# A gated delta-rule decoder layer on one core: the first normalisation pipelined over batches, head 0's key projections begun per batch

## The reference

```
xn = layernorm(x)
q, k, v = silu(causal_conv4(xn @ Wqkv))         # 16 heads of 128, 4 taps per channel
z    = xn @ Wz
beta = sigmoid(xn @ Wb);  g = softplus(xn @ Wa + dt_bias) * -exp(A_log)
per head and token:  M = exp(g) M;  M += k (v - kM) beta;  o = q M
x = x + (rmsnorm(o) * norm_w * silu(z)) @ Wout
x = x + cross attention(layernorm(x), ctx)
x = x + one of 8 experts of rank 64(layernorm(x))
```

## Time and profile before

| | |
|---|---|
| runs | 2026.42, 2033.64, 2031.08 us, median 2031.08 |
| profiled execution | span 2031.7 us from the first to the last instruction; no other time of that execution is given |
| TensorE | busy 1915.2 us, 94% of the span; mean granted clock 0.958 |
| VectorE | busy 1128.8 us, 56% |
| ScalarE | busy 934.1 us, 46% |
| GpSimd | busy 743.1 us, 37% |
| before head 0's L606 | 90.13 us, 4.4% of the span |

### The profile page before, as it was taken

One profiled execution on the slowest core, in us unless ns is written; L12 is line 12 of the kernel. 1 busy time (PEld: TensorE's weight loads), 2 busy tenths in 40 slices (PEclk: granted clock), 3 DMA queues, 4 the chain that ended last, 5 costly groups with the idle time before them and its releaser, 6 DMA issues.

```text
span 2031.7 us, 45678 instructions
## 1 busy us (share of the span) xinstructions
PE 1915.2 (94%) x16962; PEld 1561.4 (77%) x16962; DVE 1128.8 (56%) x2048; ACT 934.1 (46%) x2987; POOL 743.1 (37%) x1143
## 2 busy tenths in 40 slices
PE   5899999999999999999999998999997799999999
PEld 3688888888888888888888887888886565656574
DVE  5656565665656575656656665657563442534433
ACT  2455554646464555646464645555563321213121
POOL 1255453636363554536363535445452000000000
PEclk9899998999998999989999999989997899999999
DMA  3011111112010111111120101021114513121110
GB/s 101 16 33 32 33 40 25 34 30 42 22 38 22 38 32 33 39 25 37 28 43 22 38 22 38 23 41 34 31 24 144 146 36 93 42 83 52 55 27 21
DMA packets 220196, 87.10 MB, mean 43 GB/s; under 512 B 138320, under 2 KB 204240, under 8 KB 219280
## 3 DMA queue, kind: packets, MB, share of 16 engines
q1 hardware_dynamic: 220048, 84.83, 16.4%
HBM read 57.28 MB, written 27.53 MB: 42 GB/s over the span
## 4 chain that ended last, share of the span: by engine, by line
PE 49%; issue 25%; POOL 10%; DVE 7%; ACT 4%; DMA 3%; SPq 1%; POOLq 1%; DVEq 0%; ACTq 0%
PE bank L558 17%; PE bank L858 4%; PE bank L808 3%; DVE vT L1406 2%; POOL blkT L1774 2%; PE bank L817 2%; PE bank L770 2%; POOL prod L1770 2%; PE bank L759 2%; PE bank L678 2%; ACT vv L1074 2%; PE bank L802 2%; POOL k_tok L1740 2%; PE bank L824 1%; DMA blkT_d<-blkT 1%
## 5 line engine op out<-in xcount | busy, mean ns | idle before, releaser
L558 PE MATMUL bank<-x_hi,w_hi 128*128 128x512 f32 x1024 | 433.5, 423 | 13.4 <-DVE vT L1406 7.1
L558 PE MATMUL bank<-x_hi,w_lo 128*128 128x512 f32 x1024 | 410.3, 401 | 0.0
L558 PE MATMUL bank<-x_lo,w_hi 128*128 128x512 f32 x1024 | 408.7, 399 | 1.1 <-issue 1.1
L558 PEld LDWEIGHTS bank<-x_hi,w_hi 128*128 128x128 f32 x1024 | 197.9, 193 | 56.1 <-issue 13.9
L558 PEld LDWEIGHTS bank<-x_hi,w_lo 128*128 128x128 f32 x1024 | 196.7, 192 | 43.8
L558 PEld LDWEIGHTS bank<-x_lo,w_hi 128*128 128x128 f32 x1024 | 197.7, 193 | 33.2 <-issue 1.6
L1406 DVE SCALAR_TENSOR_TENSOR qT<-bank,cw,qT 128x511 f32<-128x511 f32 (+2 forms) x192 | 142.1, 747 | 51.1 <-ACT qT L1041 46.5
L1830 POOL TENSOR_TENSOR rstd<-ve,mhalf 128x1 f32<-128x1 f32 x32 | 17.4, 544 | 386.8 <-DVE ve L1588 386.8
L1406 DVE SCALAR_TENSOR_TENSOR kT<-bank,cw,kT 128x511 f32<-128x511 f32 (+2 forms) x192 | 143.3, 747 | 9.9 <-ACT kT L1041 4.9
L1206 ACT ACTIVATE o_tmp<-bank 128x128 f32<-128x128 f32 x256 | 67.4, 278 | 175.5 <-PE bank L824 175.5
L1406 DVE SCALAR_TENSOR_TENSOR vT<-bank,cw,vT 128x511 f32<-128x511 f32 (+2 forms) x192 | 143.2, 746 | 6.8 <-ACT vT L1041 2.3
(11 more groups left out here) (221 smaller groups left out, 4446.2 us busy)
## 6 DMA issues: line engine op xcount, KB each, us to landing
w_raw<-in_w_heads SPq DMA_DIRECT2D x64, 256.0 KB, 2.8
o_d<-og SPq DMA_DIRECT2D x64, 256.0 KB, 2.6
o_raw<-o_d SPq DMA_DIRECT2D x16, 1024.0 KB, 6.2
x_in<-in_x SPq DMA_DIRECT2D x16, 256.0 KB, 3.3
blkN_d<-nT SPq DMA_DIRECT2D x64, 64.0 KB, 2.1
t<-blkT_d SPq DMA_DIRECT2D x64, 64.0 KB, 2.4
wo_raw<-in_w_out SPq DMA_DIRECT2D x4, 1024.0 KB, 9.1
x_res<-in_x SPq DMA_DIRECT2D x16, 256.0 KB, 2.7
```

The lines of the kernel that those rows point to most:

```text
L558: last = mm(bank[bk][:, :], w[:, kind % 2, d, :], xx[:, d, b * S:(b + 1) * S], start=(n == 0), stop=(n == 3 * ND - 1))
```

## The change

- There are two input buffers: `x_in0`, and `x_in1` on the place of `nT`, which head 0 writes only later. SP loads batch 0 before the small constants, and batches 1 to 3 as the buffers come free, with the weights of K ahead of batch 1 and those of V behind it.
- DVE's `normalise_x` falls into `moments`, `normalise_x` and `low_parts`. The moments of batch b+1 stand between `x_n` and `x_lo` of batch b.
- The transposes go to banks 4 and 5; banks 0 and 1 are the jobs' from the start.
- PE runs per batch: transposes, the token transposes of the batch before, the token products, and the K job of this batch. Its K taps on ACT and K convolutions on DVE stand in the same loop, one batch behind. Weights are split at batches 0 and 1.
- The softplus chain now comes behind the convolutions of K0 to K3 on DVE. On ACT the four `silu` of K follow `tap(0, V_, 0)`.
- All loops of this stage are written out (no `Fori`).

```diff
-    x_in = s0("x_in", [P, NC, D])
+    x_in = [s0("x_in0", [P, NC, D]), at(place["nT"][0], "x_in1", [P, NC, D])]
...
+            for c in range(NC):
+                sp.dma_start(x_in[0][:, c, :], x[0, c]).then_inc(x_loaded[c], 16)
             for dst, src in ((cw_all[:, :, :, :], conv_w), (normw[:, :], norm_w), (wba[:, :, :], w_ba),
                              (alog[:, :], a_log), (dtb[:, :], dt_bias)):
                 sp.dma_start(dst, src).then_inc(small_in, 16)
...
+            def load_batch(b):
+                for c in range(NC):
+                    sp.wait_ge(stat0_step, 2 * NC * (b - 1) + c + 1)
+                    if b >= 2:
+                        sp.wait_ge(xn_done, b * NC - 2 * NC + c + 1)
+                    sp.dma_start(x_in[b % 2][:, c, :], x[b, c]).then_inc(x_loaded[c], 16)
...
             load_weight(0, K_)
+            load_batch(1)
             load_weight(0, V_)
+            load_batch(2)
+            load_batch(3)
...
-            for job in range(AHEAD):
-                if job >= 2:
-                    whole_job(0, job)
+            for b in range(B):
+                transposes(b)
+                if b == 0:
+                    pe.wait_ge(wba_split, 1)
+                else:
+                    token_transposes(b - 1)
+                token_products(b)
+                if b >= 2:
+                    whole_job(0, b)
                 else:
                     pe.wait_ge(wlo_done, 1)
-                    proj(*JOBS[job], JOB_BANK[job])
+                    proj(*JOBS[b], JOB_BANK[b])
+            token_transposes(B - 1)
+            for job in range(B, AHEAD):
+                whole_job(0, job)
...
+            split(0, K_)
+            for kind in (K_, V_, Q_):
+                taps_of(0, kind)
+            for b in range(B):
+                if b + 1 < B:
+                    high_parts(b + 1)
                 tokens(b)
+                if b == 0:
+                    split(0, V_)
+                    act.wait_ge(cw_ready, 3)
+                tap(0, K_, b)
...
+            moments(0)
+            normalise_x(0)
+            moments(1)
+            low_parts(0)
...
+            split(0, K_)
+            for b in range(1, B):
+                normalise_x(b)
+                if b + 1 < B:
+                    moments(b + 1)
+                low_parts(b)
+                if b == 1:
+                    split(0, V_)
+                tokens(b - 1)
+                conv(0, K_, b - 1)
+            tokens(B - 1)
+
+            dve.wait_ge(ba_done, B)
+            dve.wait_ge(small_in, 16 * 5)
+            chain(tt(sp_x[:, :, :], ba[:, :, H:2 * H], by_unit(dtb), ALU.add))
+            conv(0, K_, B - 1)
+            dve.wait_ge(sp_act, 5)
```

More of the change, by code:

```diff
@@ L525, in transposes, with token_products @@
                     for d in range(ND):
-                        last = tr(bank[c % 2][:, d * P:(d + 1) * P], x_n[:, c, d * P:(d + 1) * P], ident[:, :])
+                        last = tr(bank[4 + c % 2][:, d * P:(d + 1) * P], x_n[:, c, d * P:(d + 1) * P], ident[:, :])
                     last.then_inc(xtr_done, 1)
-            def tokens(b):
+            def token_products(b):
                 pe.wait_ge(xlo_done, b * NC + NC)
@@ L543, in tokens @@
                 last.then_inc(batr_done, 1)
[L545 to L550, removed]
             def proj_products(kind, b):
@@ L998, in high_parts @@
                     act.wait_ge(xtr_done, b * NC + c + 1)
-                    fn(x_hi[:, :, bass.ds(b * S + c * P, P)], grid(c % 2), ACT.Copy).then_inc(xhi_done, 1)
+                    fn(x_hi[:, :, b * S + c * P:b * S + c * P + P], grid(4 + c % 2), ACT.Copy).then_inc(xhi_done, 1)
             def tokens(b):
@@ L1365, in by_unit, with dest, conv @@
                 return v[:, :].unsqueeze(1).to_broadcast([P, UNITS, H])
+            def dest(kind, b):
+                return (kT, vT, qT)[kind][:, b, :, :].rearrange("p c t -> p (c t)")
+            def conv(h, kind, b):
+                n = conv_index(kind, b)
+                d = dest(kind, b)
+                for k in range(1, TAPS):
+                    if k == 1:
+                        dve.wait_ge(tap_done, 12 * h + n + 1)
+                    else:
+                        dve.wait_ge(conv_step, 24 * h + 2 * n + k - 1)
+                    stt(d[:, k:S], bank[JOB_BANK[JOBS.index((kind, b))]][:, 0:S - k], cw[:, kind, TAPS - 1 - k:TAPS - k], d[:, k:S],
+                        ALU.mult, ALU.add).then_inc(conv_done if k == TAPS - 1 else conv_step, 1)
+            moments(0)
+            normalise_x(0)
+            moments(1)
+            low_parts(0)
+            dve.wait_ge(wba_hi_done, 1)
+            tt(wba_lo[:, :, :], wba[:, :, :], wba_hi[:, :, :].bitcast(F32), ALU.subtract).then_inc(wba_split, 1)
+            split(0, K_)
[9 more added lines that the diff above has]
+            tokens(B - 1)
             dve.wait_ge(ba_done, B)
@@ L1700, in deviations @@
                 tt(rstd0[:, :], ve0[:, :], minus_half[:, 0:NC], ALU.pow).then_inc(rstd0_done, 1)
-            deviations(0)
-            with pool.Fori(1, B) as b:
+            for b in range(B):
                 deviations(b)
```

80 lines of the change are left out of this document (22 added, 58 removed).

## The result

The changed kernel took 2011.8 us (median of 4 runs, 2008.1 to 2019.3) against 2032.4 us (2026.4 to 2036.7) for the kernel before beside it: ratio 0.9905, 95% interval 0.9876 to 0.9934. The change gains 16 to 19 us. I had forecast 6.8 us and a time of 2024.3 us, so "faster" was right and the time lies outside the range.

What follows compares the result with a forecast made beforehand. TensorE, busy 94% of the span, was taken as the bound, only head 0's start mattering. Terms moved it from 90.13 to 82.95 us; less 0.4 for low clock, gain 6.8: span 2024.9, median 2024.3, range 2017.5 to 2032.0 us.

Steps and rivals of the forecast that it cites:

- The ring of a batch: Batches before head 0: x_n, transposes, x_hi/x_lo, token products, baT, ba in turn; 5.3 us from first transpose to first product.
- the chain from sp_x to the first convolution: Serial softplus steps after the last batch: sp_x to sp_p 3.5 us, then 7.17 to the first convolution, at 75.2 us.
- PE's wait ahead of V2: Before head 0, PE idles over 7 us for V0's convolution; V2 starts cold at 77.65 us and takes 5.3 us.
- Items 1 and 2: Batch 0: early loads bring x_n near 8.4 us; batch 1's moments cancel the 2.3 us gained; first product about 18.2.
- E: Rival: moments ahead of x_lo stall it as much as they save; in all sums for batch 0, no separate chance.
- Item 3: Block 0: 24 products together, 14 at the low clock for 6.1 us, then 10 in 2.4 us; end 26.7 us.
- Items 4 and 5: Batches 1 to 3: 11.15 us each at high clock, plus 1.65 us low-clock cost in two; K3 ends at 63.45.
- rival B: No low stretch in batches 1 to 3: gain 9.8 us, 2021.3, down to 2018 with other blocks partly fast; chance 0.22.
- Sum ahead of head 0: All terms of the prologue together put head 0's start (L606) at 82.95 us instead of 90.13.

Runs made afterwards that it cites:

- The corrected swap: Changed kernel with x_lo, wba_lo and the first weight split of batch 0 ahead of batch 1's moments on DVE, nothing else; ratio 0.9919.
- The second execution: Profiled execution of the changed kernel run again, unchanged, in the second comparison with the kernel before; ratio 0.9922, head 0 starting at 77.18 us.
- the normalisation alone: Changed kernel with K's jobs, taps, convolutions and first two weight splits back behind the batch loop; buffers, early loads and moments ahead kept; ratio 0.9927.

## Why the prediction was wrong

**Bounds and chain (right).** The ring of a batch, the chain from sp_x to the first convolution and PE's wait ahead of V2 came as written: sp_x to sp_p 3.50 us, on to the convolution 7.17, to V2 2.35 (forecast 2.45), V2 5.3.

**Items 1 and 2 (right within 0.6 us).** x_n 9.02 instead of 8.4, x_lo 13.71 instead of 13.4, first product 18.49 instead of 18.2. The early loads are cancelled by the moments of batch 1 (E). The corrected swap shows it: without them in the way the first product starts at 16.14.

**Item 3, block 0 (size off).** Seven slow products instead of fourteen: end at 25.45 instead of 26.7, 1.25 us.

**Items 4 and 5, the batches (mechanism right, size off).** A batch without a low stretch took 10.5 us twice (25.45 to 35.95; 49.00 to K3's end at 59.5), where I had 11.15. The middle one took 13.05: one low stretch and 1 us in which x_lo waited behind the moments of batch 3. Sum 34.05 against my 36.75, 2.7 us. The second execution had no low stretch in these batches, so rival B, to which I gave 0.22, was right for it: B's sum has a gain of 9.8 us, the start came 12.9 earlier (11.4 in the first, which had one low stretch). One low stretch in six such batches, where the kernel before had one in every batch, agrees with the rule of the Trainium skill (TensorE: Matmul & The Clock Gate, "What's actually happening") that activity lifts the clock, and so do the joins, with 41.1 us of low clock instead of 81.8 once products are moved into them. That the longer blocks are the reason in the batches was not tested: with the normalisation alone, whose blocks are as short as before, one low stretch was left too.

**Sum ahead of head 0.** 82.95 forecast, 78.78 and 77.18 measured. 1.25 and 2.7 make 3.95 of the 4.17 us between the first two.

**The step that failed.** Two things made the forecast of 6.8 us too small. One is the size of the low-clock terms of items 3 and 5, above: 4.2 us in the first execution, 5.8 in the second. The other is a step that had no term at all: "After L606 the streams are the same in both kernels, and PE is full there, so the change is worth what it does to the moment at which L606 starts, 90.13 us, and nothing else." The streams are the same, their places in TensorE's program are not. TensorE's stops in the joins moved with the 59 added rows, and with them the heads in which the clock falls; 5 us on average in eight comparisons come from behind the start of head 0, and the kernel that only writes the loop out has the stops of the changed kernel. The move of the stops is shown, and so is a low clock that takes about 5 us less behind the start. That the move is what makes these 5 us rests on the kernel with the loop written out alone, whose two comparisons leave 4 us, no more than the interval of each. I had seen in the windows that the clock was below 1.00 behind L606 and had not asked what puts it there. The words "if they don't, what moved them is not in this sum" name the place, but no rival had it.

**The range.** 2017.5 reached as far as rival B with a fast run. B's start and 5 us behind it make 2017 to 2018; the measured 2011.8 is lower still, by luck, as far as the runs tell: the low clock took 67 us of each of these four runs on average and 77 in the ten of the second comparison, whose median was 2017.7.

## What to carry to other kernels

A kernel that is full on TensorE still has its clock to lose: look through the windows of the whole run for stretches below 1.00 and for what TensorE did just ahead of them, before calling the rest of the run "the same". Rows added to one engine's program can move its stops in code that nobody touched; compare against a version that changes only the length before crediting the order. And where the clock falls in a thin stretch of small products, try useful large products from later in it: four a head gave 10 to 24 us in four comparisons, about as much as the whole change upstream with its 16 to 19.

## What the runs showed of the hardware

- TensorE stops for 0.3 to 2.9 us amid small products, with no wait that the profile shows: 307 stops in the heads of 18 profiles, all within two instructions of a grid with a step of 256 instructions, weight loads counted. Not every place of the grid has a stop. 59 rows more ahead (123 instructions with the loads) moved them to other heads, 60 more moved them again. What is loaded or refilled there no run shows.
- Sixty semaphore increments fit into TensorE's wait of 7.2 us; with 120 it stood 15.56 us, 130 ns for each on average.
- A product of 128x512 in plain f32 shows as two in the trace, 7.03 us for 16.
- A head at full clock takes 89.3 us, one with 10.2 us of low clock 95.1. Over the 196 heads of the 14 profiles with the joins untouched, a microsecond more at 1.2 GHz goes with 0.53 us more of the head: next to nothing in a head hides a low stretch.
- Span times mean granted clock is nearly the same in all runs of one kernel: 1947 us with a standard deviation of 2.4 in the 104 runs of the kernel before, whose spans lie between 2018 and 2046 us.
